# Delta rule: one key product for matrix and query factor, exponents a chunk ahead

## The reference, cut to what matters

```python
M = jnp.tril(-(wk_scaled @ jnp.swapaxes(wk, -1, -2)) * L_mask, -1)
A = solve_triangular(eye - M, eye, lower=True, unit_diagonal=True)
intra = jnp.tril(rk @ jnp.swapaxes(wk, -1, -2) * L_mask, -1)
def step(S, inp):
    v_new = A_i @ vsc_i - A_i @ wkd_i @ S
    o_i = rkd_i @ S + intra_i @ v_new
    S = ced_i * S + wkp_i @ v_new
```

## Time and profile before

| | us |
|---|---|
| median of 3 runs | 2408.51 (2408.32 to 2412.16) |
| the profiled execution | 2399.99 |
| its span | 2398.3 |
| delta rule, end of the stage in the span | 407.7 |
| TensorE busy, whole span | 2197.5 (92%) |
| VectorE, ScalarE, GpSimd busy | 1843.5, 1646.8, 1449.4 |

### The profile page before, as it was taken

The page is one execution under the profiler, slowest core; times in us unless marked ns, Lnnn a source line. Parts: engine busy times, 40 slices in busy tenths (PEclk is TensorE's granted clock), DMA queues, the critical chain, the costliest instruction groups (busy, mean ns, idle before and its releaser), DMA issues.

```text
span 2398.3 us, 36952 instructions
## 1 busy us (share of the span) xinstructions
PE 2197.5 (92%) x12464; PEld 1788.7 (75%) x12464; DVE 1843.5 (77%) x2832; ACT 1646.8 (69%) x2715; POOL 1449.4 (60%) x1026
## 2 busy tenths in 40 slices
PE   6799897999999999996999999999999999999986
PEld 4788796998898898884667667676676765776765
DVE  5574453667766666677989989989899899898995
ACT  6775542555555556666887788787877877888774
POOL 0236563111111113336988989889889898898895
PEclk8899998999999999997999999999999999999988
DMA  8434544566666654444655655555555555565563
GB/s 291 85 56 111 112 125 136 181 236 232 234 230 230 233 209 152 133 126 154 219 169 190 198 184 186 194 186 202 176 186 195 199 187 177 185 211 177 178 208 101
DMA packets 235434, 430.22 MB, mean 179 GB/s; under 512 B 35089, under 2 KB 117457, under 8 KB 235234
## 3 DMA queue, kind: packets, MB, share of 16 engines
q1 hardware_dynamic: 229090, 410.87, 53.0%
q0 software_dynamic: 6144, 16.79, 2.2%
HBM read 353.61 MB, written 73.96 MB: 178 GB/s over the span
## 4 chain that ended last, share of the span: by engine, by line
PE 54%; DVE 13%; issue 9%; ACT 9%; DMA 6%; POOL 6%; SPq 1%; another core or an unknown queue 1%; POOLq 1%; DVEq 0%; ACTq 0%
PE pb L1641 11%; PE pb L1614 11%; DVE pb L2094 6%; PE pb L2406 5%; PE pb L2411 5%; PE pb L994 3%; PE pb L2305 2%; PE pb L2432 2%; PE pb L2321 2%; DVE UU L2100 2%; DMA XB<-xnd 2%; PE pb L2330 2%; DMA CC<-bcd 2%; POOL UU L2019 2%; POOL UU L2027 1%
## 5 line engine op out<-in xcount | busy, mean ns | idle before, releaser
L2019 POOL TENSOR_TENSOR UU<-dx,BB 128x1024 f32<-128x1024 f32 x256 | 614.6, 2409 | 112.0 <-DMA BB<-bcd 83.6
L2231 ACT ACTIVATE pb<-dt,al 128x512 f32<-128x512 f32 x512 | 339.5, 685 | 149.4 <-DVE UU L2100 147.8
L2100 DVE TENSOR_TENSOR UU<-pb,CC 128x512 f32<-128x512 f32 x512 | 351.3, 686 | 24.3 <-DMA CC<-bcd 6.5
L2094 DVE TENSOR_TENSOR_SCAN pb<-pb,hs,UU 128x512 f32<-128x512 f32 x256 | 328.5, 1283 | 10.7 <-ACT pb L2231 7.4
L2094 DVE TENSOR_TENSOR_SCAN pb<-pb,UU 128x512 f32<-128x512 f32 x256 | 313.0, 1223 | 8.5 <-ACT pb L2231 7.9
L1381 POOL TENSOR_TENSOR clo_b<-craw_b,chi_b 128x1024 fp32r<-128x1024 f32 x22 | 62.3, 2830 | 405.9 <-ACT chi_b L1444 405.9
L1531 DVE TENSOR_TENSOR HL<-HF,HH 128x512 fp32r<-128x512 f32 x220 | 159.6, 728 | 179.9 <-ACT HH L1436 165.7
L2406 PE MATMUL pb<-HAh,WH 128*128 128x512 f32 x1024 | 282.7, 419 | 7.0 <-DVE dt L2075 5.1
L1431 ACT ACTIVATE HF<-pb,BU 128x512 f32<-128x512 f32 x192 | 132.3, 689 | 219.4 <-PE pb L1614 191.9
L2411 PE MATMUL pb<-HAl,WH 128*128 128x512 f32 x1024 | 259.7, 396 | 0.0
L1641 PE MATMUL pb<-W2h,HH 128*128 128x256 f32 x880 | 256.0, 291 | 1.0
(11 more groups left out here) (336 smaller groups left out, 4891.0 us busy)
## 6 DMA issues: line engine op xcount, KB each, us to landing
WH<-fhd SPq DMA_DIRECT2D x176, 512.0 KB, 3.5
BB<-bcd SPq DMA_DIRECT2D x256, 256.0 KB, 4.7
CC<-bcd SPq DMA_DIRECT2D x256, 256.0 KB, 5.0
raw<-in_w1a SPq DMA_DIRECT2D x23, 1024.0 KB, 7.3
raw<-in_w2a SPq DMA_DIRECT2D x23, 1024.0 KB, 7.4
craw_b<-in_fch SPq DMA_DIRECT2D x22, 512.0 KB, 5.9
fhd<-chi_b SPq DMA_DIRECT2D x22, 512.0 KB, 3.9
fld<-clo_b SPq DMA_DIRECT2D x22, 512.0 KB, 4.9
```

Of the source, the lines that this page charges most:

```text
L2019: e.tensor_tensor(ubuf(n)[:], dx[p][:], BB[n % 3][:].rearrange("p (a m) -> p a m", a=1).to_broadcast([P, 2, 512]), ALU.mult).then_inc(p_u. ...
L2094: e.tensor_tensor_scan(h_[:], h_[:], uu[:, c, :], first, ALU.mult, ALU.add).then_inc(v_sc.sem, 1)
L2100: e.tensor_tensor(uu[:, c, :], abank(n, c)[:], CC[n % 3][:], ALU.mult).then_inc(v_mu.sem, 1)
L2231: e.activation(abank(n, c)[:], dt[p][:, c, :], ACT.Exp, scale=al1[:, 2 * p + c, s:s + 1]).then_inc(c_a.sem, 1)
```

## The change

The product `kk` is made for chunk 0 only. From chunk 1 on, VectorE multiplies `kq` (one column back) by E into `MTB`, which is the matrix already turned; the transpose `MT` and ScalarE's copy go. E is therefore computed with log beta in the sums' row: a second row of sums (two more small products, `nl`, twice the broadcast). MTB and iT have two buffers each. TensorE makes `kq` of n+1 at the head of chunk n, where `kk` stood; VectorE makes iT there, behind M. On ScalarE E of n+2 comes after `rows_`, ET and ez of n+2 around the t6 copies, and the output copies follow `vn` directly. SyncE issues the sums of n+2 ahead of the blocks.

```diff
-        nm = ["rk", "ez", "wk", "vsc", "E", "ET", "MT", "Dm", "DT", "Pm", "iT", "vn", "vnt"]
+        nm = ["rk", "ez", "wk", "vsc", "E", "ET", "Dm", "DT", "Pm", "vn", "vnt"]
-        M2 = sbt("M2", [P, 2, 4, P])
+        MTB = [sbt(f"MTB{i}", [P, 2, 4, P]) for i in range(2)]
+        iTB = [sbt(f"iTB{i}", [P, 2, 4, P]) for i in range(2)]
-        cumT = sbt("cumT", [64, P])
-        ZR = [sbt(f"ZR{h}", [P, 4, P]) for h in range(2)]
+        cumT = sbt("cumT", [64, 2, P])
+        ZR = [sbt(f"ZR{h}", [P, 4, 2, P]) for h in range(2)]
-        order = ["kk'", "d4", "wkT", "wkS", "P4", "D4", "P5", "t5", "D5", "rkT''", "t6", "P6", "T6", "MT'", "vn", "v'", "o", "S", "kq'"]
+        order = ["kq'", "d4", "wkT", "wkS", "P4", "D4", "P5", "t5", "D5", "rkT''", "t6", "P6", "T6", "vn", "v'", "o", "S"]
...
@@ sp_a @@
-                    e.dma_start(ZR[h][:], cumd.rearrange(...)[n, h]....to_broadcast([P, 4, P])).then_inc(s_zr, 16)
+                    e.dma_start(ZR[h][:]...., cumd.rearrange(...)[n, h]....to_broadcast([P, 4, 2 * P])).then_inc(s_zr, 16)
...
             blocks(0)
+            sums(1)
             spread(0)
-            sums(1)
             zeros(*range(16, NZ))
             for n in range(NSEQ):
...
+                if n + 2 < NSEQ:
+                    sums(n + 2)
                 if n + 1 < NSEQ:
                     blocks(n + 1)
                 if n + 1 < NSEQ:
                     spread(n + 1)
-                if n + 2 < NSEQ:
-                    sums(n + 2)
@@ solve @@
-                    e.tensor_tensor(Y16[:, :, r:15], MB[:, r:15, :, r].rearrange("p r g -> p g r"),
+                    col = MB[:, r, :, r + 1:16] if n else MB[:, r:15, :, r].rearrange("p r g -> p g r")
+                    e.tensor_tensor(Y16[:, :, r:15], col,
@@ pool_a @@
             upper(0)
             decayed(0)
+            upper(1)
...
-                    upper(n + 1)
                     decayed(n + 1)
                     solve(e, n + 1)
+                    if n + 2 < NSEQ:
+                        upper(n + 2)
@@ dve_a @@
+            e.tensor_scalar(sm["nl"][:], sm["l"][:, :, 0:2], -1.0, None, ALU.mult).then_inc(a_dve.sem, 1)
...
-            e.tensor_copy(cumT[:], pb[6][0:64, 128:256]).then_inc(a_dve.sem, 1)
+            e.tensor_copy(cumT[:], pb[6][0:64, 128:384].rearrange("p (k t) -> p k t", k=2)).then_inc(a_dve.sem, 1)
...
             def mix(n, h):
                 W = TB[h]
-                e.wait_ge(*g_pe[h].at("kk", n))
                 e.wait_ge(*g_act[h].at("E", n))
-                if n:
-                    e.wait_ge(*g_pe[h].at("MT", n - 1))
-                    e.wait_ge(s_md, 128 * n)
-                e.tensor_tensor(M2[:, h], four(gbank("kk", n, h)), W["E"][:], ALU.mult).then_inc(g_dve[h].sem, 1)
+                if n == 0:
+                    e.wait_ge(*g_pe[h].at("kk", 0))
+                    e.tensor_tensor(MTB[1][:, h], four(gbank("kk", 0, h)), W["E"][:], ALU.mult).then_inc(g_dve[h].sem, 1)
+                    return
+                e.wait_ge(*g_pe[h].at("kq", n))
+                e.wait_ge(*(g_pe[h].at("MT", 0) if n == 1 else g_pe[h].at("P6", n - 2)))
+                e.wait_ge(s_md, 128 * (n if n == 1 else n - 1))
+                e.tensor_tensor(MTB[n % 2][:, h, :, 1:P], four(gbank("kq", n, h))[:, :, 0:P - 1], W["E"][:, :, 1:P], ALU.mult).then_inc(g_dve[h].sem, 1)
...
                     for h in range(2):
                         mix(n + 1, h)
+                    for h in range(2):
+                        inner(n + 1, h)
                 routed(n, 1)
...
                 if more:
-                    for h in range(2):
-                        inner(n + 1, h)
                     for h in range(2):
                         inverse(n + 1, h)
@@ act_a @@
+                            t = e.activation(W["E"][:, b, :], ZR[h][:, b, 1, :], ACT.Relu, bias=sm["cum"][:, n + 8 * b, h:h + 1], scale=-1.0)
...
             turned_rows(1)
             lower(1)
+            upper(1)
+            decays(1, "ET")
+            decays(1, "ez")
...
                     rows_(n + 2)
-                if more:
-                    upper(n + 1)
-                    decays(n + 1, "ET")
+                    lower(n + 2)
...
                 copy("t5", n, "t5", "DT")
                 if more:
-                    decays(n + 1, "ez")
                     carried(n + 1)
                 if n + 2 < NSEQ:
                     turned_rows(n + 2)
+                    upper(n + 2)
                 copy("t6", n, "t6", "DT")
-                if more:
-                    copy("MT", n + 1, "MT", "MT")
+                if n + 2 < NSEQ:
+                    decays(n + 2, "ET")
+                    decays(n + 2, "ez")
                 copy("vn", n, "vn", "vn")
...
-                if n + 2 < NSEQ:
-                    lower(n + 2)
                 for h in range(2):
                     e.wait_ge(*g_pe[h].at("o", n))
@@ pe_a @@
-            e.matmul(pb[6][0:64, 128:256], sm["g"][:].rearrange("p n h -> p (n h)"), utri[:], start=True, stop=True).then_inc(a_pe.sem, 1)
+            e.matmul(pb[6][0:64, 128:256], sm["g"][:].rearrange("p n h -> p (n h)"), utri[:], start=True, stop=True)
+            e.matmul(pb[6][0:64, 256:384], sm["g"][:].rearrange("p n h -> p (n h)"), utri[:], start=True, stop=False)
+            e.matmul(pb[6][0:64, 256:384], sm["nl"][:].rearrange("p n h -> p (n h)"), ident[:], start=False, stop=True).then_inc(a_pe.sem, 1)
...
                 if more:
-                    for h in range(2):
-                        e.wait_ge(*g_act[h].at("rc", n))
-                        kk(n + 1, h)
+                    inner(n + 1)
...
-                            product(f"P{l}", n, h, W["MT"], W["Dm"])
+                            product(f"P{l}", n, h, MTB[n % 2][:, h], W["Dm"])
...
-                if more:
-                    for h in range(2):
-                        MT(n + 1, h)
...
-                if more:
-                    inner(n + 1)
                 for b2 in range(2):
                     y(n, b2)
```

More of the change, by code:

```diff
@@ L198, in program @@
         ahead = ["rkT", "z", "kk", "MT", "v", "kq", "rkT'"]
-        order = ["kk'", "d4", "wkT", "wkS", "P4", "D4", "P5", "t5", "D5", "rkT''", "t6", "P6", "T6", "MT'", "vn", "v'", "o", "S", "kq'"]
+        order = ["kq'", "d4", "wkT", "wkS", "P4", "D4", "P5", "t5", "D5", "rkT''", "t6", "P6", "T6", "vn", "v'", "o", "S"]
         g_pe = [Chunks(sem(f"g_pe{h}"), ahead, order) for h in range(2)]
         g_dve = [Chunks(sem(f"g_dve{h}"), ["M", "vs", "iT", "DT"],
-                        ["M'", *(("R", "P4") if h == 0 else ("P4", "R")), "D4", "P5", "D5", "P6", "T6", "vnt", "vs'", "S", "iT'", "DT'"]) for h in range(2)]
-        g_act = [Chunks(sem(f"g_act{h}"), ["rk", "rT", "Er", "E", "ETr", "ez", "ET", "rk'", "MT", "rc", "rT'", "Er'", "E'"],
-                        ["d4", "wk", "rk''", "ETr'", "ET'", "t5", "ez'", "rc'", "rT''", "t6", "MT'", "vn", "Er''", "E''", "o"]) for h in range(2)]
-        g_pool = [Chunks(sem(f"g_pool{h}"), ["ETsel", "rkdT"], ["ETsel'", "rkdT'"]) for h in range(2)]
+                        ["M'", "iT'", *(("R", "P4") if h == 0 else ("P4", "R")), "D4", "P5", "D5", "P6", "T6", "vnt", "vs'", "S", "DT'"]) for h in range(2)]
+        g_act = [Chunks(sem(f"g_act{h}"), ["rk", "rT", "Er", "E", "ETr", "ez", "ET", "rk'", "MT", "rc", "rT'", "Er'", "E'", "ETr'", "ET'", "ez'"],
+                        ["d4", "wk", "rk''", "Er''", "E''", "t5", "rc'", "rT''", "ETr''", "t6", "ET''", "ez''", "vn", "o"]) for h in range(2)]
+        g_pool = [Chunks(sem(f"g_pool{h}"), ["ETsel", "rkdT", "ETsel'"], ["rkdT'", "ETsel''"]) for h in range(2)]
         s_md, s_mb = sem("s_md"), sem("s_mb")
@@ L316, in blocks @@
                 for q in range(8):
-                    e.dma_start(md[n, 16 * q:16 * q + 16], M2[16 * q:16 * q + 16, :, :, 16 * q:16 * q + 16]).then_inc(s_md, 16)
+                    e.dma_start(md[n, 16 * q:16 * q + 16], (MTB[n % 2] if n else MTB[1])[16 * q:16 * q + 16, :, :, 16 * q:16 * q + 16]).then_inc(s_md, 16)
             def spread(n):
@@ L558, in inner @@
                 e.wait_ge(*g_pool[h].at("ETsel", n))
-                if n:
-                    e.wait_ge(*g_pe[h].at("o", n - 1))
-                e.tensor_tensor(W["iT"][:], four(gbank("kq", n, h)), W["ET"][:], ALU.mult).then_inc(g_dve[h].sem, 1)
+                if n >= 2:
+                    e.wait_ge(*g_pe[h].at("o", n - 2))
+                e.tensor_tensor(iTB[n % 2][:, h], four(gbank("kq", n, h)), W["ET"][:], ALU.mult).then_inc(g_dve[h].sem, 1)
             def values(n, h):
@@ L870, in sums_of @@
             def sums_of(n, h):
-                return ZR[h] if n else gbank("z", 0, h)[:].rearrange("p (b m) -> p b m", b=4)
+                return ZR[h][:, :, 0, :] if n else gbank("z", 0, h)[:].rearrange("p (b m) -> p b m", b=4)
             def await_sums(n, h):
@@ L907, in decays @@
                             e.wait_ge(*g_pool[h].at("rkdT", n - 1))
```

(14 more changed lines are left out.)

18 lines of the change are left out of this document (10 added, 8 removed).

## The result

| us | kernel before | changed |
|---|---|---|
| median (8 runs each, one chip) | 2408.41 | 2421.76 |
| lowest to highest | 2397.37 to 2412.16 | 2414.26 to 2426.34 |
| profiled execution, its span | 2399.99, 2398.3 | 2421.58, 2419.8 |
| chunk 0's first transpose | 87.57 | 97.91 |
| stage ends | 407.7 | 423.7 |

The ratio is 1.0061 [1.0044, 1.0077]: slower by 13.4 us, where the forecast was -3.9 with a range up to 2416. In the profile the loop starts 10.3 us later and its eight chunks take 5.6 us more; the rest of the program differs by 5.5 between these two executions, and over all traces here it goes from 1983 to 1998, so the total is read from medians only, and a stage read from one profile is one execution's.

The account below looks back on a forecast made before the run. TensorE's order of work was taken to set an undisturbed chunk, with scatter bursts lengthening n=3 and n=5. The terms, from -12.5 for the key product to +4.5 for routing, summed to -3.9 us: median 2404.6, range 2393 to 2416.

Parts of the forecast that it names:

- One key product: TensorE, n+1 = 1 to 7: loses seven pairs of key products at 1.79 us each, -12.5 us.
- Transpose and relu: M's transpose goes but the relu delays the t6 copies: +2.7 us over n=0 to 5, -0.9 at n=6.
- the first rival, the removal comes through: The relu hides and the routing chunks gain a part: about -13.7 us, 2394.8; chance 0.22.
- Outputs copied first: ScalarE: lower(n+2) no longer precedes the output copies, so the projections' wait at 277.89 goes, -1.8 us, counted once.
- iT ahead of the routing: VectorE's chunk head: iT's products precede routing and carry; +1.0 us for n=3 to 6, +4.5 for n=1 and 2.
- Bursts at n=6: Exponents made earlier free rkdT in n=5, shifting its scatters some 4 us ahead of n=6's head: -2.0 us.
- The last chunk: n=7's end follows M, solve and 16 scatters; half of n=6's TensorE gain of 2.7 waits for the burst: +1.3.
- The start: Before the loop: sums ahead of the spread cost 2.5 us, extra matmuls and a larger copy 1.0; +3.5 us.
- exponents a chunk ahead: ET and ez of n+2 made behind t6, so GpSimd's select and rkdT no longer wait mid-chunk: -2 us.
- The spread behind the sums: At the start, first solve waits for the whole 1 MB of sums: +7.0 us, 2415.5; chance 0.18.
- the share of 0.33: DMA engines' busy share while chunk 2's sums land alone, held against the spread waiting for all the sums.

Follow-up runs that it names:

- h4: The kernel before without its 64 scatters, run in a later job than the first such run: 2355.73 us, ratio 0.9992 to the kernel before.
- h2: The changed kernel with the four routing pieces of n=2 moved late, beside the changed kernel itself: 2364.48 us, ratio 1.0024 to the kernel before.
- h3: The changed kernel with sums ahead of blocks, t6 copies ahead of relu, GpSimd's select waiting for chunk 0's DT, n=2 routing late: 2349.28 us, ratio 0.9961.
- h1: The changed kernel run once more, unedited, in a job where the kernel before took 2358.12: 2368.02 us, ratio 1.0040 to the kernel before.
- e3: The changed kernel with the t6 copies ahead of the relu of ET of n+2: 2406.98 us, ratio 1.0026 to the kernel before.
- i2: The changed kernel with the t6 copies ahead of the relu, run again in a later job: 2407.81 us, ratio 1.0020 to the kernel before.
- e2: The changed kernel with chunk 1's sums issued ahead of chunk 0's blocks: 2404.49 us, ratio 1.0010 to the kernel before.
- e4: The changed kernel with chunk 1's sums ahead of chunk 0's blocks and t6 copies ahead of the relu: 2400.42 us, ratio 1.0000 to the kernel before.
- g4: The kernel before with each of 64 scatters replaced by a plain write of the same rows in order: 2358.41 us, ratio 1.0008 to the kernel before.
- f2: The kernel before without its 64 scatters, so the experts get zeros: 2362.52 us, ratio 0.9806 to the kernel before.
- i1: The changed kernel with chunk 1's sums ahead of chunk 0's blocks and GpSimd's select waiting for chunk 0's DT: 2407.35 us, ratio 1.0022 to the kernel before.
- f4: The changed kernel with sums ahead of blocks, t6 copies ahead of relu, and scatters issued four at chunk end, eight behind M: 2410.05 us, ratio 1.0003.
- g2: The changed kernel with sums ahead of blocks, t6 copies ahead of relu, GpSimd's select waiting for chunk 0's DT, n=2 routing late: 2348.85 us, ratio 0.9967.
- e1: The changed kernel with chunk 1's sums issued behind chunk 0's spread, as before the change: 2412.62 us, ratio 1.0049 to the kernel before.

## Why the prediction was wrong

Step by step, in its own terms. Sizes are from the chunk tables where nothing else is said.

- **One key product, -12.5.** Right in its mechanism: no projection waits for OT in n=1 to n=5 of the changed kernel, TensorE has the sixteen matmuls less. Where the clock stays at 1.00 the forecast for a chunk is met: n=3 was to change by -1.79 + 0.45 + 0.25 = -1.1, and goes from 35.3 (h4) to 34.2 (h2). What the forecast did not see is that the solve's chain then stands close behind: with the relu moved as well, n=3 to n=5 gain no more (34.1, 34.1 and 33.9 in h3). The prediction had set the chain's limit at 31 us.
- **Transpose and relu, +2.7 and -0.9.** The late t6 copy was forecast to the place, and its gap measures 1.35 us. The second step that failed is what stands behind it: the sum added idle microseconds and let the products behind them run at the old speed. They did not. In h1 the clock is 0.87 to 0.95 in n=0 to n=5, and in n=3 the fall costs 3.0 us. The earlier trace rows already showed the clock at 0.92 and 0.89 in the chunks with gaps, with products of 3.78 us, and the forecast named that clock without giving it a price. In the medians this does not come out by itself: the relu's place was priced at six times 1.4 = 8.3 in the first rival, and taking it out gave 8.4 (e3) and about 9.8 (i2) across jobs and 4.1 within one (e2 to e4).
- **Outputs copied first, -1.8.** The wait in the earlier trace rows is gone, but not by the change: in g4 and h4, which keep the old order, it is 0.2 us or nothing, in f2 0.6, and in i1 and e3, which have the new order, it is back at n=4 with 2.0 and 3.7. It comes with the stalls beside the scatters, and that it was gone in the changed kernel's profile was luck.
- **iT ahead of the routing, +1.0 and +4.5.** Forecast 4.9 of waiting in n=2 (1.86 and 3.1), measured 4.49, and the chunk 3.6 longer, n=1 1.5 longer. Right. With the pieces moved, n=2 loses its 7 us, of which the medians show 3.5.
- **Bursts at n=6, -2.0.** n=6 went from 34.9 to 32.9, but product and transpose alone give that (32.7 in h4, 30.5 in h1), so nothing of this term came; and n=5, which was not in the sum, got 4.5 longer. The reason given, a threshold of about eight scatters in a row, is refuted by f4 and by g2. In such jobs stalls wander from chunk to chunk (n=4 and n=6 in e4 and i2), and their cost changes little in total: 46 us in the kernel before, about 51 in the changed one, worked out across two jobs (2408.14 times 1.0061, less 2372.04), a difference smaller than its uncertainty.
- **The last chunk, +1.3.** -0.6 in the first pair of profiles, +1.1 from h4 to h1.
- **The start, +3.5: the step that failed.** It measured +10.3. The first solve was to be 2.5 and 1.0 late and is 8.0 late. e1 takes this apart: with the sums behind the spread it is 1.0 late, as forecast for the matmuls and the copy, so the sums ahead of the spread cost 7.0 where the forecast took 2.5. Nearly all of it is issue: SyncE takes 6.9 us longer over the eight spreads. Ahead of the blocks the sums still cost 2.4 (81.57 in h3). Then 2.3 us came that no term had: GpSimd's select and product of chunk 1 now run beside VectorE's first solve. The part on "exponents a chunk ahead" looked for gains in the loop and not at what the same edit puts beside the solve at the start. i1 gives back 6.5 of the 10.3 us of start, and about 9.4 in the median.
- **The rivals.** "The spread behind the sums" had the mechanism and, at a chance of 0.18, too little weight; its deciding point of 6.4 us was passed. Of the 8 us 7.0 are the sums', 4.5 more than forecast: by the prediction's own scale that gives -3.9 + 4.5 = +0.6, no more. The clock was in no rival at all. The Trainium skill, "DMA: Bandwidth & Descriptors", section "Queues, rings and completion order", states that descriptors of one ring are consumed in order; the trace agrees with it (first use at 86.23 behind 1 MB, at 78.19 without), and the share of 0.33 in the earlier trace rows, which the forecast set against it, was the worse guide.

Put together, first in traces of the undisturbed job. From h4 to h1 the stage's end moves by 21.4 us. The start has 10.5 of them, where 3.5 were forecast. The chunks take 11.0 more, where the terms that need no stalls (-12.5 + 2.7 - 0.9 + 1.0 + 4.5 + 1.3) give -3.9: the 15 us between lie in n=0 to n=5, the chunks whose clock is under 1.00, while n=6 (-2.2) and n=7 (+1.1) are as forecast. But this is the slowest of h1's six runs against the fastest of h4's ten, and the medians are 12.3 apart; in h2's profile the clock fell behind two of the six gaps and not behind all. In the medians: the start's 6.8 and the two terms that did not come (1.8 and 2.0) bring -3.9 to +6.7, where +9.9 (h1) and +13.4 were measured; the 3 to 7 us left are what the clock's share can be there, and no run measures it alone.

The t6 copies first alone (e3, i2) and the two repairs of the start alone (i1) leave the kernel slower than before, and e2 can't be told from it; with all it is at 0.9961 [0.9947, 0.9976], 8.8 us faster. That is short of the rival "the removal comes through" (-13.7), with a start that is still 3.4 us late.

Not settled: what makes engines stand still beside the scatters in some jobs; why the clock falls behind some of the gaps of 1.35 us and not behind others; and what the repaired kernel would gain if the solve's chain were shorter.
